# Relation layer: four places packed into one register, and the first bf16 part of the records read in place

## What is computed

```python
head = entity_emb[edge_index[0]]
tail = entity_emb[edge_index[1]]
rel = relation_emb[edge_type]
att_scores = jax.nn.sigmoid(jnp.concatenate([head, rel], axis=-1) @ att_w + att_b)
neighbor_emb = att_scores * tail
aggr_emb = jax.ops.segment_sum(neighbor_emb, edge_index[0], num_segments=N_ENTITIES)
return jnp.tanh(aggr_emb @ W_w.T + W_b)
```

## Time and profile before

| | |
|---|---|
| median of 3 runs | 5188.86 us (5185.83 to 5190.13) |
| the profiled execution's own time | 5188.35 us |
| its span | 5186.5 us |
| relation layer, from the first `rec` transfer to the last matmul | 2310.3 to 2789.5 us |
| PE, DVE, ACT, POOL busy over the span | 55%, 74%, 54%, 64% |

### The profile page before, as it was taken

The page is one execution under the profiler, slowest core; times in us unless marked ns, Lnnn a source line. Parts: engine busy times, 40 slices in busy tenths (PEclk is TensorE's granted clock), DMA queues, the critical chain, the costliest instruction groups (busy, mean ns, idle before and its releaser), DMA issues. The chain is left out here.

```text
span 5186.5 us, 79200 instructions
## 1 busy us (share of the span) xinstructions
PE 2840.6 (55%) x21444; PEld 1755.7 (34%) x21445; DVE 3846.0 (74%) x8928; ACT 2821.3 (54%) x5478; POOL 3293.8 (64%) x3386
## 2 busy tenths in 40 slices
PE   7777777777777777727777533333333333333335
PEld 7644444444444444417776311111111111111124
DVE  8999988888888888837876266666666666666654
ACT  4166666666666666612223366666666666666633
POOL 0167777777777777774001477777777777777762
PEclk9555555555555555557776555555555555555555
DMA  5222222222222222227662344444444444444421
GB/s 71 61 79 85 85 85 85 85 85 85 85 83 78 84 85 85 82 70 154 126 126 43 94 117 120 122 116 123 123 123 123 123 123 121 116 120 118 120 64 21
DMA packets 669069, 505.15 MB, mean 97 GB/s; under 512 B 566237, under 2 KB 583005, under 8 KB 668868
## 3 DMA queue, kind: packets, MB, share of 16 engines
q1 hardware_dynamic: 550868, 246.86, 19.9%
q0 software_dynamic: 108640, 196.86, 13.0%
q10 hardware_dynamic: 9360, 59.56, 3.0%
HBM read 289.86 MB, written 213.16 MB: 97 GB/s over the span
## 5 line engine op out<-in xcount | busy, mean ns | idle before, releaser
L612 POOL DMA_INDIRECT records<-rec,place x1612 | 1554.8, 965 | 745.8 <-issue 467.4
L1324 POOL DMA_INDIRECT got_a<-kv_table,idx_a x1612 | 1561.9, 969 | 501.8 <-issue 488.5
L849 DVE SCALAR_TENSOR_TENSOR same_before<-p_src,src_f,before 128x128 bf16<-128x128 f32 x1612 | 773.1, 533 | 0.0
L1340 PE MATMUL p_a<-ident,flat_attr 128*128 128x128 f32 x434 | 123.4, 431 | 832.5 <-ACT flat_attr L1377 790.5
L698 ACT ACTIVATE lo_away<-p_lo,minus_number 128x512 bf16<-128x512 f32 x434 | 285.2, 657 | 444.5 <-PE p_lo L653 444.5
L655 PE MATMUL p_src<-fields,select 3*128 3x512 bf16 x434 | 250.0, 576 | 402.7 <-DVE same_before L849 402.3
L1349 PE MATMUL p_a<-relu,w_t 128*128 128x512 f32 x248 | 230.9, 1035 | 419.3 <-DVE relu L1459 363.9
L994 PE MATMUL acc<-high,lo_r 128*128 128x64 bf16 x1708 | 344.5, 244 | 124.6 <-issue 87.2
L640 PE MATMUL p_h<-window,dst_hot 128*128 128x64 bf16 x4836 | 330.5, 239 | 146.0 <-ACT h_gated L717 123.2
L630 PE MATMUL p_look<-table_low,lo_hot_t 128*128 128x98 bf16 x1612 | 410.0, 281 | 0.0
L630 PE MATMUL p_look<-table_rest,lo_hot_t 128*128 128x98 bf16 x1612 | 409.4, 280 | 0.0
(11 more groups left out here) (361 smaller groups left out, 8575.6 us busy)
## 6 DMA issues: line engine op xcount, KB each, us to landing
sums<-packed_a ACTq DMA_DIRECT2D x62, 936.0 KB, 3.9
q_starts<-zero_q SPq DMA_DIRECT2D x62, 884.0 KB
rec_r<-records SPq DMA_DIRECT2D x124, 442.0 KB, 5.1
qin<-q_starts SPq DMA_DIRECT2D x62, 884.0 KB, 6.9
attr_a<-records SPq DMA_DIRECT2D x62, 442.0 KB, 5.0
records<-rec,place POOLq DMA_INDIRECT x1612
got_a<-kv_table,idx_a POOLq DMA_INDIRECT x1612
stage<-in_edge_attr SPq DMA_DIRECT2D x61, 416.0 KB
```

The costliest lines, as they stand in the source:

```text
L612: nc.gpsimd.indirect_dma_start(k.records, bass.IndirectOffsetOnAxis(ap=place[b][:, t:t + 1], axis=0), rec[b][:, t, :], None).then_inc(s_se ...
L849: last = v.scalar_tensor_tensor(same_before[:, first:first + j + 1, :].rearrange("p g e -> p (g e)"), p_src[:, 0:(j + 1) * P], k.src_f[:, ...
L1324: nc.gpsimd.indirect_dma_start(got[b][:, t, :], None, k.kv_table, bass.IndirectOffsetOnAxis(ap=idx[b][:, t:t + 1], axis=0)).then_inc(s_got ...
```

## The change

Three things are changed.

1. At the end of `sort`, DVE makes the block numbers as floats, packs four of them into one number of base 64, multiplies it by 64 and writes 7 integers for each turn (`WORDS`) instead of 26. PE loads 7 registers in place of 26 and takes each place out of them with a shift and an AND.
2. ACT's copy `high` is gone. The first part is the upper half of the words of the record itself, truncated and not rounded, read in place by both PE (`top`) and DVE (`upper(of)`); `rest` is the record minus that half. The semaphores `s_in` and `s_high`, which tied ACT to DVE and PE, are gone.
3. Since PE now reads `rec`, SP waits on `s_used` (PE is through with chunk n - 2) before it overwrites the buffer, where it waited on `s_rest`.

```diff
@@ sort, DVE, at its end
-                    e.mark(v.tensor_scalar(k.to_at[:, half], p_look[b][0:1, 0:NS // 2], 0.5, None, ALU.mult))
+                    e.mark(v.tensor_scalar(block_of[:, half], p_look[b][0:1, 0:NS // 2], 1.0 / P, None, ALU.mult))
+                e.mark(v.memset(padded[:], 0.0))
                 e.wait()
+                e.then(v.tensor_copy(padded[:].rearrange("p c w e -> p c (w e)")[:, :, 0:2 * TS], block_of[:].rearrange("p (c j) -> p c j", j=2 * TS)))
+                held = padded[:].rearrange("p c w e -> p (c w) e")
+                e.then(v.scalar_tensor_tensor(word[:], held[:, :, 3], float(D), held[:, :, 2], ALU.mult, ALU.add))
+                e.then(v.scalar_tensor_tensor(word[:], word[:], float(D), held[:, :, 1], ALU.mult, ALU.add))
+                e.then(v.scalar_tensor_tensor(word[:], word[:], float(D), held[:, :, 0], ALU.mult, ALU.add))
+                e.then(v.tensor_scalar(k.to_at[:], word[:], float(D), None, ALU.mult))
@@ relation_layer
-        high = [tile(f"high{b}", [P, T, D], BF16) for b in range(2)]
+        def upper(of):
+
+            return of.rearrange("p t c -> p (t c)").bitcast(BF16).rearrange("p (t c e) -> p t c e", c=REC, e=2)[:, :, :, 1]
@@ SP
-                        wait(sp, s_rest, 2 * i + b - 1)
+                        wait(sp, s_used, 2 * i + b - 1)
@@ PE
-                def add(n, b, tiles, to):
-                    pe.wait_ge(s_high, n + 1)
+                def add(n, b, of, tiles, to):
                     pe.wait_ge(s_split, n + 1)
+                    top = upper(of)
...
-                        for part in (high[b][:, t, :], mid[:, t, :, 1], low[b][:, t, :]):
+                        for part in (top[:, t, H0:REC], mid[:, t, :, 1], low[b][:, t, :]):
...
-                    at = nc.values_load_multi_w_load_instructions(
-                        k.to_at[0:1, bass.ds(i * 2 * TS, 2 * TS)], engines=[mybir.EngineType.PE], min_val=0, max_val=D * (HI - 1),
+                    words = nc.values_load_multi_w_load_instructions(
+                        k.to_at[0:1, bass.ds(i * WORDS, WORDS)], engines=[mybir.EngineType.PE], min_val=0, max_val=D ** (HELD + 1) - 1,
...
+                    def block_at(j):
+
+                        held = (words[j // HELD] >> (BITS * (j % HELD))) & (D * (D - 1))
+                        return held.with_bounds(min_val=0, max_val=D * (HI - 1))
+
                     for b in range(2):
-                        add(2 * i + b, b, T, lambda j: bass.ds(at[b * TS + j], D))
+                        add(2 * i + b, b, rec[b][:], T, lambda j: bass.ds(block_at(b * TS + j), D))
@@ ACT
-                def copy(n, b, of, tiles):
-                    act.wait_ge(s_in, n + 1)
-                    wait(act, s_used, n - 1)
-                    nc.scalar.copy(high[b][:, 0:tiles, :], of[:, :, H0:REC]).then_inc(s_high, 1)
...
@@ DVE, split
-                    dve.sem_inc(s_in, 1)
                     c.mark(v.tensor_tensor(lo[b][:, :, 0:tiles], k.iota_b[:, :, 0:tiles], bc(rel[b][:, 0:tiles], 1, P), ALU.is_equal))
-                    dve.wait_ge(s_high, n + 1)
-                    v.tensor_tensor(rest[b][:, 0:tiles, :], of[:, :, H0:REC], high[b][:, 0:tiles, :], ALU.subtract).then_inc(s_rest, 1)
+                    v.tensor_tensor(rest[b][:, 0:tiles, :], of[:, :, H0:REC], upper(of)[:, :, H0:REC], ALU.subtract).then_inc(s_rest, 1)
```

More of the change, by code:

```diff
@@ L50 @@
 SECOND = HI - 1
+HELD = 4
+WORDS = -(-2 * TS // HELD)
+BITS = (D - 1).bit_length()
 S2 = 12
@@ L53 @@
 EPS = 1e-5
-assert TS * SUPER == T and S2 * SECONDS == SECOND and S2 <= TS
+assert HI <= D == 1 << BITS and TS * SUPER == T and S2 * SECONDS == SECOND and S2 <= TS
 assert CHUNKS * T == NT and PAIRS * 2 == CHUNKS == FULL + 1 and P * T < E and P <= ROWS
@@ L540, in sort @@
         pair_f = tile("pair_f", [HI, NS])
+        block_of = tile("block_of", [1, NS])
+        padded = tile("padded", [1, PAIRS, WORDS, HELD])
+        word = tile("word", [1, PAIRS * WORDS])
         begun = tile("begun", [HI, NS], BF16)
@@ L915, in relation_layer @@
         zeros = tile("zeros_r", [1, 512], BF16)
-        s_zero, s_second, s_idx, s_got, s_in, s_high, s_rest, s_split, s_used, s_all, s_dve, s_passed, s_ends = (
-            sem(n + "_r") for n in ("s_zero", "s_second", "s_idx", "s_got", "s_in", "s_high", "s_rest", "s_split", "s_used",
+        s_zero, s_second, s_idx, s_got, s_rest, s_split, s_used, s_all, s_dve, s_passed, s_ends = (
+            sem(n + "_r") for n in ("s_zero", "s_second", "s_idx", "s_got", "s_rest", "s_split", "s_used",
                                     "s_all", "s_dve", "s_passed", "s_ends"))
@@ L997, in body @@
                 def body(i):
-                    at = nc.values_load_multi_w_load_instructions(
-                        k.to_at[0:1, bass.ds(i * 2 * TS, 2 * TS)], engines=[mybir.EngineType.PE], min_val=0, max_val=D * (HI - 1),
-                        skip_runtime_bounds_check_because="a sum of at most HI - 1 steps of D, made on the chip")[1]
+                    words = nc.values_load_multi_w_load_instructions(
+                        k.to_at[0:1, bass.ds(i * WORDS, WORDS)], engines=[mybir.EngineType.PE], min_val=0, max_val=D ** (HELD + 1) - 1,
+                        skip_runtime_bounds_check_because="HELD block numbers below D, one after the other, times D, made on the chip")[1]
+                    def block_at(j):
+                        held = (words[j // HELD] >> (BITS * (j % HELD))) & (D * (D - 1))
+                        return held.with_bounds(min_val=0, max_val=D * (HI - 1))
                     for b in range(2):
-                        add(2 * i + b, b, T, lambda j: bass.ds(at[b * TS + j], D))
+                        add(2 * i + b, b, rec[b][:], T, lambda j: bass.ds(block_at(b * TS + j), D))
                 loop(pe, body)
@@ L1006, in _ @@
                 for m in range(SECONDS):
-                    add(CHUNKS + m, m % 2, tiles2, lambda j: slice((m * S2 + j + 1) * D, (m * S2 + j + 2) * D))
+                    add(CHUNKS + m, m % 2, second_rows(m), tiles2, lambda j: slice((m * S2 + j + 1) * D, (m * S2 + j + 2) * D))
                 pe.wait_ge(s_used, CHUNKS + SECONDS)
@@ L1815, in build @@
             k.base2 = tile("base2", [P, HI])
-            k.to_at = tile("to_at", [1, NS], I32)
+            k.to_at = tile("to_at", [1, PAIRS * WORDS], I32)
             k.idx2 = tile("idx2", [P, HI], I32)
```

## The result

The changed kernel takes 5289.59 us (median of 4 runs, 5288.4 to 5291.65) against 5187.99 us before: ratio 1.0196, 95% interval 1.0179 to 1.0214. It is slower, by 102 us. The forecast was 5289 us. The profiled execution's span is 5286.6 us against 5186.5.

What follows compares the result with a forecast made beforehand. A chain of hand-overs bounds the layer; SP's new wait puts one buffer's split, matmuls and transfer in line. 5188.35 + 97.5 (30 turns, 17.71 against 14.46 us) + 3 (early rounds) = 5288.9, forecast 5289 us, range 5262 to 5322.

Steps and rivals of the forecast that it cites:

- What bounds the kernel: Relation layer: no engine full, a chain of hand-overs bounds it; 14.46 us a turn, 2.5 of it PE's register loads.
- The step from the earlier trace: SP's queue: SP waits 273.3 us for `rest`, yet DVE waits for no transfer, since transfers are wholly covered.
- The round of one buffer: Record buffers under SP's new wait: split, matmuls and transfer follow one another, 17.71 us a turn against 14.46, 97.5 us.
- The start: Some 5 rounds while `second` is gathered: slower landing now counts, 0.4 to 1.8 us each, 0.6 taken, 3 us.
- The register load: PE, between turns: 7 words take some 0.84 us, bounds 0.44 and 6.4, covered by PE's gap of 6.3 us.
- The faster rival: Relation layer: transfer stays covered and DVE becomes the bound, 11.96 us a turn, 5113 us; chance 4%.
- Register arithmetic: PE's shifts and ANDs: taken as hidden under matmuls; rival: not hidden, 0.96 us more a chunk, 5318 us, 8%.
- The shorter transfer: Release to landing: rival of 4.55 us, turn 16.41 us, 5250 us; skill's fit gives about 5240 us; chance 6%.
- The clock: PE's granted clock may fall; costs nothing, as a chunk's matmuls took 5.41 us at 0.50 and 5.38 at 1.00.
- The packing in `sort`: Before the layer: five more DVE operations, a few us, covered by DVE's 62.64 us of idle time; cost nothing.

Runs made afterwards that it cites:

- two runs with 28 words a turn: Kernel before with a turn's 26 places stored 28 words apart: loads from multiples of 16 bytes, 5124.90 us; places one word further, 5241.42 us.
- the one never aligned: Kernel before with 26 places stored 28 words apart and one word further, so no load begins at a multiple of 16 bytes: 5241.42 us.

## Why the prediction was right

**What bounds the kernel.** The step from the earlier trace rows was right: a wait of SP that costs nothing today because it is released early enough. The run with SP's wait alone shows it without any other part of the change.

**The round of one buffer**, term by term, means over the last 50 record chunks of the trace after: split 5.94 us (predicted 6.04; the handshake with ACT was in it), `low` to the first matmul 0.23 and 0.34 for the two chunks of a turn (0.28), matmuls 5.39 (5.39), release to landing 0.18 + 5.74 = 5.92 (5.85), landing to `rel` 0.23 and 0.13 (0.15). The sum is 17.70 and 17.73 us; 17.71 was predicted. Some of that closeness is luck: the split was 0.1 us too long and the landing 0.07 us too short. The step between the two chunks of a turn was expected at 6.0 us and is 6.33 us, since DVE waits for the second chunk's transfer as well; the round of a buffer doesn't depend on it.

**The start.** I gave the rounds beside the gathering of `second` 0.6 us more each. In the trace the first four rounds of each buffer are 18.1 to 19.5 us long, 0.4 to 1.8 us more, just the bounds that I had named. With a mean turn of 17.83 us the loss in 30 turns is 101.1 us, against 100.5.

**The register load.** This term was wrong in size: 0.84 us predicted, 1.06 us in each fourth turn and 1.70 us in the others. I had drawn a line through one word and the fast load of 26, and had left the slow ones at 6.4 us as a bound without asking why they alternate. The two runs with 28 words a turn put it down to the start address: 7 words are 28 bytes a turn, a multiple of 16 bytes in one turn of four. It did no harm here, since PE's gap of 6.2 us covered either, but it made the "faster" rival's price wrong.

**The faster rival.** I gave 5113 us for a covered transfer with DVE as the bound. The mechanism exists, and four buffers show it; the time is 5117.6 us with the load as it is and 5110.0 us with a quick load. For a kernel with ACT's copy 11.96 us a turn was too low by 0.17 us: I had taken 5.98 us for both steps of a turn. With 8 words the step over the turn's edge is 5.97 us, but the one between its two chunks is 6.15 us, since DVE still waits a little for PE there.

**Register arithmetic.** 1395 single and 806 fused register operations in place of 806 fused ones, and the matmuls of a chunk still last 5.39 us: hidden, as predicted, for 2.7 of them to each pair of tiles. What remains in sight stands in front of a chunk's first matmul: 0.23 and 0.34 us behind `low`, where reading in place with 26 registers has 0.13 us. The turn gains nothing by that: `rel` follows the landing by 0.34 us there, in place of 0.23 and 0.13, and why stays open.

**The shorter transfer.** The mean from first issue to landing was 5.74 us, as in the row that I had used. The 4.1 us estimated from the fit in the Trainium skill (DMA: Bandwidth & Descriptors, Anatomy of one DMA) did not come about: the measured time is 1.6 us longer.

**The clock.** The granted clock fell from 0.71 to 0.63 of full speed in the stretch from 2400 to 2750 us, and the matmuls of a chunk took 5.39 us in both. It cost nothing.

**The packing in `sort`.** DVE's idle time before the layer shrank from 62.64 to 58.9 us, by the operations added. They were covered.

## What to carry to other kernels

A copy that looks superfluous may be what lets a buffer go. Before a later engine is made to read a buffer in place, write down who releases it then, add up the round of that one buffer (fill, every reader in line, release), and compare it with the turn: 17.7 us against 14.5 us said here that either the copy stays or the buffers double. And judge each part of a change by itself: the packing, worth 62 us alone, was sunk by the reading in place, which alone costs 100.

## What the runs showed of the hardware

The time of a load of registers from SBUF depends on where it starts and on the number of words. The start is counted here from the first byte of `to_at`. 26 words take 2.1 us from a multiple of 16 bytes, and 6.2 us from 4 or 8 bytes behind one; 7 words take 1.06 us from a multiple and 1.70 us from 4, 8 or 12 bytes behind one. 8 words, 32 bytes a turn, take 0.59 us; one word, on SP, takes 0.44 us in the median. Off the multiples this is 0.24 us a word. In every kernel but the one never aligned the layer's first load starts at the first byte: 2.34 us for 26 words, 1.28 us for 7 and 0.78 us for 8. So 8 words are quicker than 7 from the same start. Pieces of several words followed by single ones would explain it (26 and 7 leave a remainder, 8 doesn't), but that reading is only argued.

A chunk of matmuls with 64 columns and a weight load for each takes the same time at a granted clock of 0.50 and of 1.00, 0.069 us for each matmul; what sets that pace stays open.
